# Routed experts of a mixture layer: a lead slot beside the weight ring, results kept in two blocks used in turn, three ends of experts in one word

## What is computed

```python
x = x + xattn(layernorm(x), ctx, ctx, mask, ...)
h = layernorm(x).reshape(-1, 256)               # 2048 tokens
shared_out = (silu(h @ sg) * (h @ su)) @ sd     # 256 -> 512 -> 256, all tokens
topk_ids = argmax(h @ gate_w, -1)               # one of 32 experts
xs = h * sigmoid(max(h @ gate_w, -1))[:, None]
order = argsort(topk_ids); sorted_x = xs[order]
g = ragged_dot(sorted_x, routed_gate_w, tokens_per_expert)
u = ragged_dot(sorted_x, routed_up_w, tokens_per_expert)
d = ragged_dot(silu(g) * u, routed_down_w, tokens_per_expert)
return x + shared_out + d[argsort(order)]
```

## Time and profile before

| what | value |
|---|---|
| three runs | 293.36 us median, 292.28 to 294.63 |
| the profiled execution's own time | 291.1 us |
| its span, first to last instruction | 289.2 us |
| mean granted TensorE clock | 0.972 of full speed |
| PE busy | 250.5 us (87%) |
| DVE busy | 163.1 us (56%) |
| ACT busy, POOL busy | 94.0 us, 87.9 us |
| DMA | 68.69 MB, 238 GB/s over the span |
| routed loop, first gate matmul to last down matmul | from 130.00 us, to about 255.6 us |

### The profile page before, as it was taken

One profiled execution on the slowest core, in us unless ns is written; L12 is line 12 of the kernel. 1 busy time (PEld: TensorE's weight loads), 2 busy tenths in 40 slices (PEclk: granted clock), 3 DMA queues, 4 the chain that ended last, 5 costly groups with the idle time before them and its releaser, 6 DMA issues.

```text
span 289.2 us, 12925 instructions
## 1 busy us (share of the span) xinstructions
PE 250.5 (87%) x4627; PEld 184.6 (64%) x4629; DVE 163.1 (56%) x490; ACT 94.0 (33%) x284; POOL 87.9 (30%) x248
## 2 busy tenths in 40 slices
PE   4997899997799899998979999999999999698800
PEld 3765666553375358856867888788788787543700
DVE  0655796878469543016656667666666667424333
ACT  2344875454230110235323333334333333211000
POOL 1262221111005777102222223222222222103772
PEclk9996899999999999999999999999999999999985
DMA  6999994000001325401998869999999999733565
GB/s 196 328 394 410 404 401 157 2 2 1 2 0 37 109 96 165 160 16 50 329 390 286 300 236 331 358 410 415 416 410 411 415 412 409 312 83 94 174 214 164
DMA packets 32559, 68.69 MB, mean 238 GB/s; under 512 B 3966, under 2 KB 18715, under 8 KB 32539
## 3 DMA queue, kind: packets, MB, share of 16 engines
q1 hardware_dynamic: 25723, 61.60, 56.4%
q0 software_dynamic: 1536, 4.20, 4.7%
q10 hardware_dynamic: 5280, 2.62, 3.5%
HBM read 59.49 MB, written 8.91 MB: 237 GB/s over the span
## 4 chain that ended last, share of the span: by engine, by line
PE 66%; DMA 9%; DVE 8%; issue 5%; POOL 5%; ACT 3%; POOLq 1%; SPq 1%; ACTq 1%; DVEq 0%
PE bank L1039 23%; PE bank L961 14%; PE bank L1061 11%; DMA ring_gu<-n_L_ffn_routed_up_w_dram 5%; PE bank L973 5%; POOL xs_flat L463 5%; PE bank L874 3%; PE bank L926 2%; PE bank L909 2%; DMA slot_rows<-late 2%; DVE h_place L531 1%; ACT h_place L749 1%; DVE h_place L532 1%; DMA h_place<-in_L_xattn_kernel_q_dram 1%; DMA xs_flat<-slot_rows,slot_i 1%
## 5 line engine op out<-in xcount | busy, mean ns | idle before, releaser
L1039 PE MATMUL bank<-ring_gu,x_c 128*32 128x128 f32 x2528 | 86.8, 275 | 6.6 <-issue 2.6
L1039 PEld LDWEIGHTS bank<-ring_gu,x_c 128*32 128x32 f32 x2528 | 64.8, 109 | 20.3 <-issue 8.1
L1061 PE MATMUL bank<-ring_d,h_place 128*32 128x128 f32 x1264 | 51.8, 274 | 2.3 <-issue 1.6
L646 DVE TENSOR_TENSOR h_place<-h_place,bank 128x128 f32<-128x128 f32 x79 | 31.2, 395 | 33.2 <-PE bank L1039 30.9
L456 POOL COPY x_c<-xs_flat 128x32 f32 x79 | 16.6, 210 | 101.2 <-PE bank L1039 88.5
L1061 PEld LDWEIGHTS bank<-ring_d,h_place 128*32 128x32 f32 x1264 | 36.1, 109 | 7.7 <-DVE h_place L651 5.3
L792 ACT COPY late<-bank 128x128 f32 (+1 forms) x79 | 21.0, 266 | 57.5 <-PE bank L1061 57.5
L973 PE MATMUL bank<-shd,h_place 128*128 128x256 f32 x128 | 28.4, 380 | 2.1 <-DVE h_place L532 2.1
L651 DVE STREAM_TRANSPOSE h_place<-h_place 128x128 f32<-128x128 f32 x79 | 24.6, 311 | 9.9 <-PE bank L1061 1.7
L787 ACT ACTIVATE h_place<-bank 128x128 f32<-128x128 f32 x79 | 21.9, 277 | 23.6 <-PE bank L1039 19.3
L531 DVE SCALAR_TENSOR_TENSOR h_place<-h_place,bank 128x512 f32<-128x512 f32 x16 | 11.0, 686 | 32.5 <-ACT h_place L749 32.5
(11 more groups left out here) (132 smaller groups left out, 261.9 us busy)
## 6 DMA issues: line engine op xcount, KB each, us to landing
ring_gu<-L_ffn_routed_gate_w_dram SPq DMA_DIRECT2D x32, 512.0 KB, 9.4
ring_gu<-n_L_ffn_routed_up_w_dram SPq DMA_DIRECT2D x32, 512.0 KB, 10.3
ring_d<-L_ffn_routed_down_w_dram SPq DMA_DIRECT2D x32, 512.0 KB, 10.3
slot_rows<-late ACTq DMA_DIRECT2D x10, 256.0 KB, 6.5
x<-in_x_dram SPq DMA_DIRECT2D x4, 512.0 KB, 7.3
slot_rows<-zeros SPq DMA_DIRECT2D x1, 2048.0 KB, 20.4
late<-sorted_rows SPq DMA_DIRECT2D x8, 256.0 KB, 3.4
out_dram<-x SPq DMA_DIRECT2D x8, 256.0 KB, 2.4
```

The costliest lines, as they stand in the source:

```text
L646: v.tensor_tensor(h_r.rearrange("p (m f) -> p m f", m=KF), g_silu.rearrange(rows, m=KF), bank[1][:, 0:P].rearrange(rows, m=KF), ALU.mult). ...
L1039: ins = te.matmul(bank[g][q * LW:(q + 1) * LW, 0:P], x_c[:, k], ring_gu[:, s, g, k, q * P:(q + 1) * P], start=(k == 0), stop=(k == KD - 1))
L1061: ins = te.matmul(bank[2][r:r + LW, 0:DH], hT[:, f * LW:(f + 1) * LW], ring_d[:, s, f, a * DH:(a + 1) * DH], start=(m == 0), stop=(m == HA ...
```

## The change

1. The ring of `ring_gu` and `ring_d` gets a seventh slot, LEAD. It holds expert 0 and is never refilled. Experts 1 to 6 stand in slots 0 to 5, so seven experts are loaded at the start. `refill` still waits for expert e and loads expert e + 6, now for e from 1 to 25 (it was 0 to 25).
2. `y_halves` has room for 32 chunks, two blocks used in turn; the index of a chunk is masked with 31 (ACT L799, DVE L665 in the new numbering). ACT waits at chunk 1 of a block, and once before the last block, until the block before the last one has landed in DRAM (`y_stored`, with a credit of 32). `never_early` and its fill are gone.
3. The ends of experts are packed, in words of 8-bit parts: the first two in `first_ends`, the other 30 in ten words of three in `ends`. DVE packs them with multiply-add operations, two of which wait for the one ahead. PE loads one word, of three ends, at the switch to every third expert, and takes each end out with shift and mask.
4. In PE's order the load stands between gate and up; it stood between up and down. The rest after the rounds is one expert.

```diff
+    LEAD = RING
+    Y_RING = 2 * STORE
-    ROUNDS = NE // RING
-    REST = NE % RING
+    ROUNDS = (NE - 2) // RING
+    PACK = 3
+    PACK_BITS = 8
...
-        y_halves = late[:, 0:SLOTS * DH].rearrange("p (c d) -> p c d", c=SLOTS)
+        y_halves = late[:, 0:Y_RING * DH].rearrange("p (c d) -> p c d", c=Y_RING)
...
-            for s in range(RING):
-                load_gate_up(s, s)
-                load_down(s, s)
+            for e, s in enumerate((LEAD, *range(RING))):
+                load_gate_up(e, s)
+                load_down(e, s)
...
             with sp.Fori(0, ROUNDS - 1) as it:
                 for s in range(RING):
-                    refill(RING * it + s, s)
-            for s in range(REST):
-                refill(RING * (ROUNDS - 1) + s, s)
+                    refill(RING * it + s + 1, s)
+            refill(RING * (ROUNDS - 1) + 1, 0)
...
-            g_.memset(never_early, 0.0)
...
-            v.memset(turn[:, 0:1], 1).then_inc(table_ready, 1)
-            v.tensor_scalar(turn[:, 1:NE + 1], chunk_cum[0:1], 1.0, None, ALU.add).then_inc(table_ready, 1)
+            step(v.tensor_scalar(turn[:], chunk_cum[0:1], 1.0, None, ALU.add))
+            v.scalar_tensor_tensor(out=first_ends[:], in0=turn[:, 1:2], scalar=float(1 << PACK_BITS), in1=turn[:, 0:1],
+                                   op0=ALU.mult, op1=ALU.add).then_inc(table_ready, 1)
+            packs = turn[:, 2:NE].rearrange("p (k j) -> p k j", j=PACK)
+            step(v.scalar_tensor_tensor(out=packs[:, :, 1], in0=packs[:, :, 2], scalar=float(1 << PACK_BITS),
+                                        in1=packs[:, :, 1], op0=ALU.mult, op1=ALU.add))
+            v.scalar_tensor_tensor(out=ends[:], in0=packs[:, :, 1], scalar=float(1 << PACK_BITS),
+                                   in1=packs[:, :, 0], op0=ALU.mult, op1=ALU.add).then_inc(table_ready, 1)
...
-                sums = y_all[:, bass.ds(c, 1)].rearrange("p c d -> p (c d)")
-                other = y_halves[HR:P, bass.ds(c, 1)].rearrange("p c d -> p (c d)")
+                sums = y_all[:, bass.ds(c & (Y_RING - 1), 1)].rearrange("p c d -> p (c d)")
+                other = y_halves[HR:P, bass.ds(c & (Y_RING - 1), 1)].rearrange("p c d -> p (c d)")
...
-                              y_all[a * LW:(a + 1) * LW, bass.ds(STORE * b, STORE)]).then_inc(y_stored, 16)
+                              y_all[a * LW:(a + 1) * LW, bass.ds((b & 1) * STORE, STORE)]).then_inc(y_stored, 16)
...
                 for j in range(STORE):
+                    if j == 1:
+                        act.wait_ge(y_stored, HALVES * 16 * b)
                     silu(STORE * b + j)
                     take_y(STORE * b + j - 1)
...
+            act.wait_ge(y_stored, HALVES * 16 * blocks)
             with act.Fori(STORE * blocks, n_chunks) as c:
...
-                other_chunks(w, end, s, 16 * it + 16)
-                w, end = next_expert(end, RING * it + s, s, 16 * it + (16 if s + 1 < RING else 32))
+                n = (s + 1) % RING
+                other_chunks(w, end, s, d_landed)
+                pe.wait_ge(gu_in[n], gu_landed if n else gu_landed_next)
+                gate(end, n)
+                if s % PACK == 0:
+                    packed = packed_ends(ends[0:1, bass.ds((RING // PACK) * it + s // PACK, 1)], PACK)
+                w, end = end, end_in(packed, s % PACK)
+                up(w, n)
+                down_of(w, s)
```

More of the change, by code:

```diff
@@ L141, in build_cross_attention_moe @@
         mask_b = mask_flat.rearrange("p (b i k) -> p b i k", b=B, i=NTB)
-        never_early = late[0:HR, late_taken[0]:]
         x1 = sb("x1", [P, NT, D])
@@ L190, in build_cross_attention_moe @@
         begin = sb("begin", [1, P], I32)
-        turn = sb("turn", [1, NE + 1], U16)
+        turn = sb("turn", [1, NE])
+        first_ends = sb("first_ends", [1, 1], I32)
+        ends = sb("ends", [1, (NE - 2) // PACK], I32)
         block_n = sb("block_n", [1, 1], I32)
@@ L216, in build_cross_attention_moe @@
         shared_in = sem("shared_in")
-        gu_in = [sem(f"gu_in{s}") for s in range(RING)]
-        d_in = [sem(f"d_in{s}") for s in range(RING)]
+        gu_in = [sem(f"gu_in{s}") for s in range(RING + 1)]
+        d_in = [sem(f"d_in{s}") for s in range(RING + 1)]
         zeros_out = sem("zeros_out")
@@ L458, in _ @@
                 g_.tensor_copy(x_c[:, 1], xsT[:, 1, bass.ds(col, LW)]).then_inc(x1_part, 1)
-            pool.wait_ge(y_stored, HALVES * 16 * (blocks + 1))
+            pool.wait_ge(y_stored, HALVES * 16 * (blocks + 2))
             pool.sem_inc(pool_waited, 1)
@@ L1066, in _, with packed_ends, end_in @@
             n_chunks = chunk_count(pe)
-            def turn_of(e):
-                return nc.values_load(turn[0:1, bass.ds(e, 1)], engines=(mybir.EngineType.PE,), min_val=1, max_val=MAX_CHUNKS + 1,
-                                      skip_runtime_bounds_check_because="unsigned, a running sum of chunks with at least one for each expert")
+            def packed_ends(ap, n):
+                return nc.values_load(ap, engines=(mybir.EngineType.PE,), min_val=0, max_val=(1 << n * PACK_BITS) - 1,
+                                      skip_runtime_bounds_check_because="each part is masked where it is taken out")
+            def end_in(packed, j):
+                return pe.snap((packed >> (PACK_BITS * j)) & ((1 << PACK_BITS) - 1))
             def other_chunks(w, end, s, landed):
```

70 lines of the change are left out of this document (34 added, 36 removed).

## The result

The changed kernel takes 296.92 us (median of 20 runs, 293.22 to 301.64), the kernel before 294.03 us (20 runs beside it, 291.12 to 297.96). The ratio is 1.0106, with a 95% interval of 1.0073 to 1.0138: slower by 1%, where 292.8 us and no change were forecast. Medians count all runs; ratios leave out those over 1.5% above their kernel's fastest. The profiled execution took 295.28 us (span 293.4), against 291.1 us (span 289.2) before.

The account below looks back on a forecast made before the run. A gapless train of weight transfers starting at PE's chunk 30 was taken to end the routed loop. Terms -1.0 + 0.5 + 0.6 - 0.8 + 0.1 gave -0.6 us: from median 293.36 to 292.8 us, range 290.6 to 294.8 us.

Parts of the forecast that it names:

- part (5): PE's 1.59 us stall for its code at 146.8 us: stays (0), goes (-1.6) or a second appears (+1.6); -0.8 us taken.
- Part (1): Lead slot: only expert 6's load leaves the routed loop, prefetch depth is the same; 0 us, bound 3.9 us.
- rival A: The lead slot does shorten the train of weight transfers by 3.9 us, giving 288.9 us; chance 0.14.
- Part (2): PE's loads of ends: 11 left, switches without one gain 0.2 us each, five ahead of chunk 30, -1.0 us.
- Part (3): DVE's packing near 94 us: two more table operations with waits on the path ahead of the residual, +0.5 us.
- Part (4): Masks in the chunk loop: free on ACT, half showing on DVE in 12 inner chunks, +0.6 us.
- rival B: DVE's chunk loop takes the pace through the added register operation, +3.3 instead of +0.6 us, 296.3 us; chance 0.11.
- Part (6): Removed fill on POOL, 5.04 us at 111.9 us, ends 13 us before the first gate needs POOL: 0 us.
- Part (7): Two blocks in turn: ACT's wait for stores has about 2 us of room; 0 us, bound +1 us.
- rival D: A store is not down in time and ACT holds silu, using more than the end's slack; about 294.5 us, chance 0.06.
- Part (8): Tail: four stores at the end with two more register operations on their way, +0.1 us.
- Rival C: The round's code no longer fits what PE holds and is fetched each round: 9 more stalls, 14 us, 307 us; chance 0.02.

Follow-up runs that it names:

- held kernels: Kernel before with expert 7's refill and those behind it held until chunk 10's (in one, chunk 9's) products are done: ratios 0.9976, 0.9927 and 0.9869.
- Both packing experiments: Changed kernel with one end loaded per expert again, ratio 1.0136 to the kernel before; kernel before with ends packed three a word alone, ratio 0.9982.
- second hold: Changed kernel with expert 10's refill held until chunk 18's gate and up products are done: ratio 1.0134 to the kernel before.
- before again: The kernel before, unchanged, run and profiled a second time: ratio 1.0018 to the kernel before.

## Why the prediction was wrong

**The failing step is part (5).** It named the place, the mechanism and the rival outcome ("a second one can appear"), and then took -0.8 us, because "the new code puts each expert nearly at the same place in the program, a slot later". The step that I didn't take was to ask which experts make the first pass, and which inner loops they enter there: the slot later is the point. Slot 5's inner loop, which expert 5 with its one chunk skipped, is now entered by expert 6 with seven, in the first pass. What it costs: chunk 18 at 4.19 and 3.92 instead of 1.50 and 1.49, +2.6 us. That is more than my +1.6 us bound, which was one old stall as one execution had shown it; with the old stall, chunk 11 is at 1.9 to 3.3 in the kernel before and at 2.7 to 4.7 in the kernel after. The load of expert 6, now gone, was not what the stall queued behind: in the held kernels it goes as ever, and the halt is down to 0.2 to 0.6 us. The stated range missed the same thing: its upper end, 294.8 us, is 293.36 + 0.8 + 0.6 and leaves out part (5)'s own +1.6 us, with which it would have been 296.4 us.

Going by the two profiles of each kernel, the added time sums up thus: chunk 0 +0.4; chunk 11 +1.2 (by chance or not, two and two executions don't tell); chunk 18 +2.6; chunks 19 and 20 +0.6, from the half-clock stretch of one execution; the other chunks ahead of 30 +0.2; middle +0.1; chunks 74 to 78 -0.1; tail +0.4. That makes 5.4 us between the mean spans, 294.3 and 288.9 us. The medians of all runs differ by 2.9 us, so the profiled pairs show the gap large. The 2.6 us of the new stall come near the whole of it, but the two blocks alone cost 1.6 us (0.5 to 2.8) by their ratio, so how the 2.9 us divide between the two is not settled: no kernel here has the whole change and neither the new stall nor held refills. The mean granted clock over the runs compared is no part of it, 0.966 after (13 runs) and 0.965 and 0.970 for before in two jobs.

**Part (1)** was right in its sum and incomplete in its reach. No weights are saved from the train. But the lead slot does something else: it shifts which expert meets which code. The rival A fell: from chunk 30 to expert 31 the first profiles differ by 0.15 us.

**Part (2)** was right on the bound and wrong on the size. The loads, line 1081:

```profile
L1081 PEldq FUSED_REGOPS  x10: 52/52/57, 140.3 to 247.9; - x10
L1081 PEldq TENSOR_LOAD <-ends x10: 298/304/322, 140.4 to 248.0; - x10
L1081 PEldq TENSOR_LOAD <-first_ends x1: 321/321/321, 130.3 to 130.3; - x1
```

There are 11, as said. But a switch without one takes 1.51 to 1.61 us, where the switches inside a round took 1.58 to 1.67 us before and 1.4 us was named as the sign. And the chunk behind a switch with a load, 1.34 us before, now takes 1.46 us or more, which gives part of the gain back. Both packing experiments say 0.05 us a switch or less; 0.2 was forecast. PE's waits at experts 30 and 31 did not grow to 4 or 5 us as the forecast had it: they are 1.37 and 0.40 us, since PE gains next to nothing inside the train.

**Part (3)** was right, +0.5 us. The chain:

```profile
93.64 0.17 DVE chunk_end L626
93.81 0.10 DVE turn L627
...
93.93 0.15 DVE first_ends L628
94.08 0.09 DVE turn L631
...
94.19 0.16 DVE ends L633
94.35 1.20 DVE x L539 x2
```

From chunk_end to the residual 0.71 us, before 0.19 us. Chunk 0 is at 130.1 and 130.8 us, against 130.0 and 130.1 us.

**Part (4)** was right in size: the two blocks cost 0.65 us in the 44 chunks of the middle, 0.015 us each, so some 0.45 us ahead of chunk 30 where 0.6 was taken. By its second ratio the kernel with the two blocks alone costs 1.6 us, where these pieces make 1.1 us; its interval holds both. The inner chunks stay at 1.34 to 1.36 us, so rival B, DVE's pace, fell. **Part (6)**: POOL is 5.4 us less busy from 97 to 130 us, PE's 32.37 us are the same, so 0 was right. **Part (7)**: PE has no wait on the stores that shows, and rival D had no part in it. **Part (8)** was too low, +0.4 us instead of +0.1. In the chain the last store's issue on ACT took 0.86 us before and 2.18 us after, and the transfer behind it 5.12 and 3.81 us, so the two together are the same, 5.98 and 5.99 us. What has grown is the work on ACT ahead of them: the end of PE's last matmul to the start of POOL's first gather is 8.5 us before and 8.8 us after.

**Rival C** had the right matter and the wrong rounds. The forecast had its own sign for it, packets on the instruction queue between 160 and 250 us, and one came, at 163.8 us, still in the first pass (a second instruction queue, q14, has one at 237.4 us; whose it is isn't shown). Rounds 2 to 5 stay free of stalls. The rule cited from the Trainium skill ("Runtime: NRT & Kernel Launch", "Instruction fetch mechanics") misled in two ways: a stall at each jump back is not what any of these traces shows, and the same section of the Trainium skill has the crossing into the next block of code as "mostly hidden", where these traces show halts of up to 3.35 us beside such a block's packet. I had used the rule's failure for the rounds to set the matter aside, when code that has not run yet was what bore on the change.

## What to carry to other kernels

Count the first pass of unrolled code as a resource with traffic of its own: a change that adds a slot, or moves which work meets which copy of the code first, can put a stall of 2 to 3 us wherever weights stream at the same time. Test such a suspicion by holding the transfers, not by touching the engine's program: one wait on the issuing engine took each stall away by itself, all or most of it. And where a long train of transfers sets the end, hold it only where it has slack; a hold of 7 to 8 us in the kernel before gained 0.7% in the one of three measurements that is clear of noise with twelve runs, while one of 18 us in the changed kernel, with all refills behind it, took it from 1% slower than before to 2%.

## What the runs showed of the hardware

The chip's instruction packets come late beside weight traffic. Over all kernels, chunk 11 came at 1.49 to 2.24 in the five profiles in which no weights moved ahead of it, and at 2.74 to 5.07 in twelve of the thirteen others. The thirteenth is the second profile of before, at 1.89, with a DMA share of 0.83 from 144 to 147 us: its instruction packet starts at 144.72 us, in the first profile at 145.96 us. So the traffic makes a halt likely and not certain.

The packets also say where the time goes. In all 19 halts of PE of over 1 us in the routed loop with no semaphore behind them, in thirteen profiles, PE goes on 1.2 to 1.7 us after the end of a 16 KB packet on q8. The packet itself is not slower at the new tear, 0.93 us in the changed kernel and in its second hold alike; what moves is its start, at 158.61 us just as the halt begins, and with the weights held at 159.12 us, 2.1 us before PE ran out. So the time is lost ahead of the packet. Whether the sequencer asks later or the packet queues isn't seen in its start; only the traffic differs between these two kernels. In each kernel the halt falls at the same place of the program.

The granted clock falls to half (1.2 of 2.4 GHz) in stretches that come and go between executions of one program. Between 76 and 82 us, a place with no change in any kernel, before, before again and the held kernel's second profile read, in this order:

```profile
76.00:82.00 6.00, 4.26 (x11) 2.14 (x13) 2.98 (x10) 1.66 (x6) 0.19 (x1) 1.00 0.00 0
```

```profile
76.00:82.00 6.00, 5.86 (x11) 2.61 (x13) 1.64 (x9) 0.48 (x1) 0.00 (x0) 0.72 0.00 0
```

```profile
76.00:82.00 6.00, 5.43 (x17) 3.13 (x18) 3.15 (x11) 1.48 (x4) 0.33 (x2) 1.00 0.00 0
```

One such stretch moves the first chunk by a microsecond or more (130.1 us in the second of these against 128.85 us in the third; the first has its chunk 0 at 130.0 us with none here but a longer stretch from 24 us on). A single pair of profiles can therefore not settle a difference of 1%.

In the routed loop the stretches are not spread at random. From 84 to 265 us the eighteen profiles have nine of them, and each begins within 1.4 us of the end of an idle time of PE of 1.8 to 3.4 us, a halt or a wait for weights; but 18 of 27 such idle times are followed by none. So the stretch at 162 us in the first profile of the changed kernel may well be a consequence of the new stall, one that comes in some executions and not in others: the second profile has the stall without it. No run here tests that.
